# Cross attention of a Perceiver block: the keys computed by seven half-size products and kept in DRAM, in place of scores straight from the context

## The chip, the cores and the metric

The kernel runs on one core of one Trainium2 chip. The metric is the device time of one execution in microseconds (us); times compared are medians of several executions.

## What is computed

The reference is a two-layer model on x (8 batches x 64 rows x 512) with a context of 8 x 1601 rows x 1024. Only this part of it matters here, the cross attention of the second layer (16 heads of 64, one learned null key and value in front of or behind the 1601 others):

```
q      = layernorm(x) @ Wq                      # 512 -> 1024, 16 heads x 64
k, v   = split(context @ Wkv, 2)                # 1024 -> 2 x 1024
k, v   = k, v with the null key / null value    # 1602 keys per batch
p      = softmax(q @ k.T / 8)                   # per batch and head: 64 x 1602
out    = (p @ v) @ Wout
```

Every large product is made of float16 parts: a float32 operand is a high half plus a low half (the rest), and a product is high x high + high x low + low x high, three matmuls.

## The kernel before

The program is a row of stages: depool, Mamba, BitNet, `queries` (stage "cq"), `attend` (stage "ca"), then `project_out`, `head_attention`, `experts`. One engine program stands per stage and engine, in a fixed order, tied by semaphores.

**Values.** V = context @ Wv for all batches is computed ahead, as filler between the work of the early stages (`ValueWork`) and at full width in `queries` (`QuadWork`: two tiles of 128 context rows by the two halves of the width, as seven products of half-size blocks in place of eight, the sums and differences made on GpSimd and VectorE), split into halves and written to DRAM (`vd`). 17 such quads run in `queries`.

**Scores, in `attend`.** The keys are never formed. The loop runs over f = 0 to 63: 8 batches x 8 pairs of heads. `project(f, r)` (L1820 to L1822) multiplies the pair's query by Wk transposed, so that the query is 1024 wide (24 matmuls of 128 columns, moved by L1911 on ScalarE and L1964 on VectorE into `qw`); `chunk(f, n)` (L1841 to L1843) multiplies it with the split context, in four chunks of 448, 448, 353 and 352 keys, eight slices of the width and three matmuls for each: 96 matmuls. The context halves of one batch lie in three rings of `ctx` (`halves` and `ctx`); the tiles of the next batch are loaded (L1750), split on ScalarE (L1905) and on VectorE (L1957) while this one is used. Wk transposed is prepared in `queries` (items "keyw"), and so are the first seven tiles of batch 0 (`load_first`, `first_high`, `first_low`, L701 and L705).

**After the scores**, per pair: `peak_of` and `offset` on VectorE (L1969, L1973: the maximum), `exps` on ScalarE (L1919), `inverse` (L1978, L1981), `weights_high` on ScalarE (L1928), `weights_low` on VectorE (L1986), `turn` on the queue of SyncE (L1769: two DMA transposes of the two halves), and `attend_to` on TensorE (L1870, L1873) with the pair's values, loaded by L1757 and L1759; every fourth pair `leave` (L1995, L1997) moves the sums out of PSUM. `attend_to(f - 2)` stands between the chunks of f, so TensorE has a pair and a half of other work while the weights of a pair are made. `probs` and `parts` have one buffer each, the scores six banks of PSUM.

## Time and profile before

| | us |
|---|---|
| median of 3 runs | 3063.41 (3062.07 to 3064.23) |
| the profiled execution | 3065.92 |
| its span | 3063.9 |
| TensorE busy in the span | 2838.0 (93%) |
| VectorE, ScalarE, GpSimd busy | 1625.4, 1041.0, 248.5 |
| `attend`: first matmul to the last sum moved out | 1331.5 to 2583.9 |
| granted TensorE clock, mean | 0.967 |

The profile is of one execution. PE is TensorE's matmul, PEld its weight load, DVE VectorE, ACT ScalarE, POOL GpSimd, SP SyncE (SPq its queue of DMA issues). A matmul's duration in the trace includes its way through the array, so two that follow each other overlap: what one costs is the distance between two starts. The clock is given in tenths or as a share of full speed (2.4 GHz).

### The profile page before, as it was taken

What the parts mean: (1) busy time and instruction counts of PE and PEld (TensorE: products, weight loads), DVE (VectorE), ACT (ScalarE), POOL (GpSimd) and SP (SyncE); (2) the same over time, 40 slices, a digit from 0 to 9 for tenths busy, and PEclk for the clock granted to TensorE, in tenths of its full rate; (3) what the DMA queues carried; (4) which work ended last, traced back from release to release, by engine and by line L of the source; (5) the groups of instructions that cost most, each with busy time, mean ns of one, the idle gap of its engine ahead of it and who ended that gap; (6) DMA issues with size and microseconds to landing.
All of it is one profiled execution on the core that took longest, in us unless ns stands there. A gap on an engine that the chain in (4) does not pass through costs nothing. (4 is left out here: it accounts for less than half of the span.)

```text
span 3063.9 us, 42939 instructions
## 1 busy us (share of the span) xinstructions
PE 2838.0 (93%) x17913; PEld 1507.4 (49%) x17921; DVE 1625.4 (53%) x1942; ACT 1041.0 (34%) x1621; POOL 248.5 (8%) x338
## 2 busy tenths in 40 slices
PE   6999999998989999989999999999999997786799
PEld 3334444443444444446665666666666664334453
DVE  5358999995565666643434343434343432367410
ACT  2254433431433443332333333333232321173210
POOL 1000000000000555500000000000000000100000
PEclk9999999999999999999999999999999998887899
DMA  5033334334323444345655565555555544100203
GB/s 203 24 108 103 96 108 129 94 97 163 126 83 126 146 128 139 113 129 116 146 117 143 117 149 116 149 115 150 115 150 114 130 86 104 59 7 22 110 21 131
DMA packets 487175, 343.00 MB, mean 112 GB/s; under 512 B 246884, under 2 KB 452005, under 8 KB 482759
## 3 DMA queue, kind: packets, MB, share of 16 engines
q1 hardware_dynamic: 486982, 340.26, 40.8%
q8 instruction: 142, 2.33, 0.3%
q14 instruction: 51, 0.41, 0.0%
HBM read 231.06 MB, written 54.62 MB: 93 GB/s over the span
## 5 line engine op out<-in xcount | busy, mean ns | idle before, releaser
L1841 PE MATMUL ca_p_s<-early_halves,ca_qw 128*128 128x448 f16 (+2 forms) x1408 | 466.7, 331 | 1.4 <-DVE ca_qw L1964 1.4
L1843 PE MATMUL ca_p_s<-early_halves,ca_qw 128*128 128x448 f16 (+2 forms) x1408 | 466.8, 332 | 0.0
L1842 PE MATMUL ca_p_s<-early_halves,ca_qw 128*128 128x448 f16 (+2 forms) x1408 | 466.8, 332 | 0.0
L1964 DVE TENSOR_TENSOR ca_qw<-ca_p_w,ca_qw 128x512 f16<-128x512 f32 x128 | 88.5, 691 | 508.3 <-ACT ca_qw L1911 508.3
L394 PE MATMUL vw_pv<-vw_wv,vw_ctx 128*128 128x512 f16 (+1 forms) x688 | 263.9, 384 | 36.6 <-PEq L74 15.3
L395 PE MATMUL vw_pv<-vw_wv,vw_ctx 128*128 128x512 f16 (+1 forms) x688 | 263.6, 383 | 0.0
L396 PE MATMUL vw_pv<-vw_wv,vw_ctx 128*128 128x512 f16 (+1 forms) x688 | 263.6, 383 | 0.0
L1911 ACT ACTIVATE ca_qw<-ca_p_w 128x512 f16<-128x512 f32 x128 | 76.4, 597 | 504.5 <-PE ca_p_w L1822 504.5
L1842 PE MATMUL ca_p_s<-ca_ctx,ca_qw 128*128 128x448 f16 (+2 forms) x640 | 216.2, 338 | 0.0
L1841 PE MATMUL ca_p_s<-ca_ctx,ca_qw 128*128 128x448 f16 (+2 forms) x640 | 216.1, 338 | 0.0
L1843 PE MATMUL ca_p_s<-ca_ctx,ca_qw 128*128 128x448 f16 (+2 forms) x640 | 216.1, 338 | 0.0
L1919 ACT ACTIVATE ca_probs<-ca_p_s,ca_small 128x896 f32<-128x896 f32 (+1 forms) x128 | 117.6, 924 | 219.5 <-DVE ca_small L1973 219.5
L1843 PEld LDWEIGHTS ca_p_s<-early_halves,ca_qw 128*128 128x128 f16 x1408 | 137.9, 98 | 99.1 <-issue 0.9
L1986 DVE SCALAR_TENSOR_TENSOR ca_parts<-ca_probs,ca_small,ca_parts 128x1602 f16<-128x1602 f32 x64 | 120.8, 1888 | 118.6 <-ACT ca_parts L1928 118.6
L1841 PEld LDWEIGHTS ca_p_s<-early_halves,ca_qw 128*128 128x128 f16 x1408 | 137.8, 98 | 90.5 <-DVE ca_qw L1964 1.7
L1842 PEld LDWEIGHTS ca_p_s<-early_halves,ca_qw 128*128 128x128 f16 x1408 | 137.8, 98 | 88.8 <-issue 0.9
L1248 ACT ACTIVATE work<-early_halves,mb_a_neg 128x252 f32<-128x252 f32 x256 | 104.7, 492 | 219.2 <-DVE ms_h L1281 215.5
L1969 DVE TENSOR_REDUCE ca_small<-ca_p_s 128x1 f32<-128x896 f32 (+1 forms) x128 | 126.5, 988 | 64.3 <-PE ca_p_s L1843 64.3
L394 PE MATMUL ms_pv<-vw_wv,vw_ctx 128*128 128x512 f16 x336 | 129.2, 385 | 16.8 <-DVE vw_ctx L370 8.6
L1281 DVE TENSOR_TENSOR_SCAN ms_h<-work,ms_h 128x2048 f32<-128x2048 f32 x32 | 141.3, 4417 | 0.0
L1806 POOL COPY ca_q_diag<-work 64x128 f16<-64x128 f16 x128 | 43.9, 343 | 1158.7 <-PE ca_p_s L1843 1154.8
L394 PEld LDWEIGHTS vw_pv<-vw_wv,vw_ctx 128*128 128x128 f16 (+1 forms) x688 | 67.7, 98 | 128.5 <-issue 27.5
(554 smaller groups left out, 5356.6 us busy)
## 6 DMA issues: line engine op xcount, KB each, us to landing
ca_stage<-in_ctx_t SPq DMA_DIRECT2D x97, 512.0 KB, 3.6
vd<-vw_vst SPq DMA_DIRECT2D x192, 256.0 KB, 2.3
ca_vals<-vd SPq DMA_DIRECT2D x64, 768.0 KB
vw_ring<-in_ctx_t SPq DMA_DIRECT2D x89, 512.0 KB, 3.8
ex_w_d<-in_w_d SPq DMA_DIRECT2D x8, 2048.0 KB, 7.2
vw_ring<-in_w_kv SPq DMA_DIRECT2D x16, 512.0 KB, 4.7
early_r<-state_rows SPq DMA_DIRECT2D x8, 1024.0 KB, 7.7
early_r<-in_w SPq DMA_DIRECT2D x2, 4096.0 KB, 14.3
```

The source lines that it names most:

```text
L394: self.nc.tensor.matmul(o, xh[:, c, 0:w], self.wv[0][:, c, f], start=(c == 0), stop=False)
L395: self.nc.tensor.matmul(o, xh[:, c, 0:w], self.wv[1][:, c, f], start=False, stop=False)
L396: last = self.nc.tensor.matmul(o, xl[:, c, 0:w], self.wv[0][:, c, f], start=False, stop=(c == CC - 1))
L1248: ins = nc.scalar.activation(da[q][:, m, :, 1:], steps, ACT.Exp, scale=a_neg[:, e, q * NQ + m:q * NQ + m + 1])
L1281: nc.vector.tensor_tensor_scan(flat, da[q].rearrange("p n b s -> p (n b s)"), flat, 0.0, ALU.mult, ALU.add).then_inc(scanned, 1)
L1841: nc.tensor.matmul(o, a[:, 0, c, :], x[:, 0, c, lo:hi], start=(c == 0), stop=False)
L1842: nc.tensor.matmul(o, a[:, 0, c, :], x[:, 1, c, lo:hi], start=False, stop=False)
L1843: last = nc.tensor.matmul(o, a[:, 1, c, :], x[:, 0, c, lo:hi], start=False, stop=(c == CC - 1))
L1919: nc.scalar.activation(probs[:, CUTS[2 * h]:CUTS[2 * h + 2]].rearrange("p (a n) -> p a n", a=2), scores(f, h), ACT.Exp, bias=nbias, scale= ...
L1964: nc.vector.tensor_tensor(qw[f % 2][:, 1, c, :], p_w[:, :].rearrange("p (c n) -> p c n", n=P), qw[f % 2][:, 0, c, :], ALU.subtract).then_i ...
L1969: nc.vector.tensor_reduce(peak[:, h:h + 1], scores(f, h), AX.XY, ALU.max).then_inc(peak_done, 1)
L1986: nc.vector.scalar_tensor_tensor(parts[:, 1, 0:KEYS], probs[:, :], rinv, parts[:, 0, 0:KEYS], ALU.mult, ALU.subtract).then_inc(wl_done, 1)
```

## The change

K itself is computed, in `attend`, by a new class `KeyWork`. A batch's 1602 keys are four quads of two tiles of 201 keys (198 in the last). A quad's K is seven products of half-size blocks instead of eight: each has 4 blocks of 128 features x 4 slices of the width x 3 matmuls of 201 columns, 48 matmuls, so 336 matmuls per quad and 32 quads. GpSimd makes four sums of 804 columns and four low halves per quad, ScalarE seven high halves, VectorE three low halves; the products are added up on VectorE (14 additions of 402 columns) with two copies by ScalarE (`keep`), split (four `out_high`, four `out_low`) and written to DRAM (`kd`). A step t of the new order is half a quad (seven groups of 24 matmuls, `kw.pe`) together with one pair of heads f = t - 9: `load_keys` reads the pair's keys back, `score(f)` is 12 matmuls of 402 (396) columns from the 128-wide query itself, and `attend_to(f - 1)` follows. Products run in steps 0 to 63, pairs in steps 9 to 72. The scores have four banks of PSUM instead of six, the products three. `project`, `chunk`, `null_of`, the splitting of context tiles and the six-bank rotation are gone, and so are "keyw" and the first tiles in `queries`; there a new class `KeyWeights` makes the seven half-size weight blocks in eight steps spread over 16 quads (56 high halves, 56 low halves and 32 subtractions of 256 columns).

The core of the diff:

```diff
+KQ = 4
+KN = 201
+KN_LAST = KEYS // 2 - (KQ - 1) * KN
...
             self.add(dve, i, 0)
+            if step and not later:
+                keys.low_given(dve, s)
+            elif step:
+                keys.low(dve, s, 3)
+                keys.low(dve, s, 4)
+                keys.second(dve, s)
...
+class KeyWeights:
+    ORDER = [0, 3, 5, 2, 4, 1, 6]
+    WIDE = BANK // 2
+    STEPS = CC // 2 * 2
...
+    def low_given(self, dve, s):
+        w11, w12, w21, w22 = self.quarters
+        for n in range(3):
+            self.low(dve, s, n)
+        dve.wait_ge(self.lo, 7 * s + 3)
+        self.nc.vector.tensor_tensor(w11, w12, w11, ALU.subtract).then_inc(self.made, 1)
+        dve.wait_ge(self.made, 4 * s + 1)
+        self.nc.vector.tensor_tensor(w12, w22, w12, ALU.subtract).then_inc(self.made, 1)
...
+class KeyWork:
+    SLOTS = 9
+    STAGED = 3
+    BANKS = 3
+    QUADS = B * KQ
+    HALF = CC // 2
+    WIDE = HALF * KN
+    OF_SUMS = {2: 0, 1: 1, 4: 2, 5: 3}
+    BY_POOL = [1, 2, 4, 5]
+    BY_DVE = [0, 3, 6]
...
+    def load(self, sp, i):
+        if i >= self.QUADS:
+            return
+        if i:
+            sp.wait_ge(self.op_lo, 3 * i)
+            sp.wait_ge(self.s_lo, 4 * i)
+        for t in range(2):
+            sp.dma_start(self.raws[t][:, :, :].rearrange("p h n -> p (h n)"),
+                         self.io.ctx_k[i // KQ, i % KQ, t, :, :]).then_inc(self.ld[t], 16)
...
+        g.tensor_tensor(s[:, 0, :], b[:, 0, :], b[:, 1, :], ALU.add).then_inc(self.s_made, 1)
+        g.wait_ge(self.s_made, 4 * i + 1)
+        g.tensor_tensor(s[:, 1, :], s[:, 0, :], a[:, 0, :], ALU.subtract).then_inc(self.s_made, 1)
+        g.wait_ge(self.s_made, 4 * i + 2)
+        g.tensor_tensor(b[:, 0, :], a[:, 0, :], b[:, 0, :], ALU.subtract).then_inc(self.s_made, 1)
+        g.wait_ge(self.s_made, 4 * i + 3)
+        self.low_of_sum(g, i, 1)
+        g.wait_ge(self.s_lo, 4 * i + 1)
+        self.low_of_sum(g, i, 2)
...
+        g.wait_ge(self.s_lo, 4 * i + 2)
+        self.low_of_sum(g, i, 4)
+        g.wait_ge(self.s_lo, 4 * i + 3)
+        g.tensor_tensor(self.sums[:, 0, :], self.raws[0][:, 1, :], self.sums[:, 1, :], ALU.subtract)\
+            .then_inc(self.s_made, 1)
+        self.low_of_sum(g, i, 5)
...
+    def pe(self, pe, m):
+        i, r, h = m // 14, m % 14 // 2, m % 2
+        if h == 0:
+            if r in self.BY_POOL:
+                pe.wait_ge(self.s_lo, 4 * i + self.BY_POOL.index(r) + 1)
+            else:
+                pe.wait_ge(self.op_lo, 3 * i + self.BY_DVE.index(r) + 1)
+        if m >= self.BANKS:
+            j, q, g = (m - self.BANKS) // 14, (m - self.BANKS) % 14 // 2, (m - self.BANKS) % 2
+            if q:
+                pe.wait_ge(self.added, 14 * j + self.ADD_AT[self.READ[q], g] + 1)
+            else:
+                pe.wait_ge(self.copied, 2 * j + g + 1)
+        w, x, o, n = self.tk[r], self.slot(i, r), self.bank(m), self.wide(i)
+        for e in range(2):
+            f = slice((2 * h + e) * P, (2 * h + e + 1) * P)
+            for c in range(self.HALF):
+                k = slice(c * KN, c * KN + n)
+                self.nc.tensor.matmul(o[:, e, :], w[:, 0, c, f], x[:, 0, k], start=(c == 0), stop=False)
+                self.nc.tensor.matmul(o[:, e, :], w[:, 0, c, f], x[:, 1, k], start=False, stop=False)
+                last = self.nc.tensor.matmul(o[:, e, :], w[:, 1, c, f], x[:, 0, k], start=False, stop=(c == self.HALF - 1))
+        last.then_inc(self.prod, 1)
...
+            def load_keys(f):
+                b, p = divmod(f, PAIRS)
+                if p == 0:
+                    kw.landed(sp, b)
+                if f >= 2:
+                    sp.wait_ge(scored, 2 * (f - 1))
+                o = keys[f % 2]
+                source = kd[b, :, :, p, :, :].rearrange("q t p n -> p (q t) n")
+                sp.dma_start(o[:, 0:2 * KQ - 1, :, :].rearrange("p a l n -> p a (l n)"), source[:, 0:2 * KQ - 1, :])\
+                    .then_inc(ld_k[f % 2], 16)
...
+            for t in range(STEPS):
+                f, (i, later) = t - BEHIND, divmod(t, 2)
+                if t and not later:
+                    kw.load(sp, i + 1)
+                if 0 <= f + 1 < NF:
+                    load_keys(f + 1)
+                if t < PARTS and later:
+                    kw.out(sp, i, 0)
+                if f >= 0:
+                    turn(f, 0)
+                    turn(f, 1)
+                if t < PARTS and later:
+                    kw.out(sp, i, 1)
+                    kw.out(sp, i, 2)
+                if 2 <= f + 1 < NF:
+                    load_values(f + 1)
+                if t < PARTS and later:
+                    kw.out(sp, i, 3)
...
+            def score(f):
                 pe.wait_ge(q_ready, 2 * f + 2)
-                if 2 * f + r:
-                    pe.wait_ge(qw_low, 2 * f + r)
-                p, q = f % PAIRS, q_diag[f % 2]
-                for i in range(CC // 2):
-                    c = (r * CC // 2 + i) * P
-                    o = p_w[:, i * P:(i + 1) * P]
-                    nc.tensor.matmul(o, wkt[0][:, p, c:c + P], q[:, 0, :], start=True, stop=False)
-                    nc.tensor.matmul(o, wkt[0][:, p, c:c + P], q[:, 1, :], start=False, stop=False)
-                    last = nc.tensor.matmul(o, wkt[1][:, p, c:c + P], q[:, 0, :], start=False, stop=True)
-                last.then_inc(qw_ready, 1)
-            def chunk(f, n):
-                b, h = f // PAIRS, n // 2
-                if n % 2 == 0:
-                    if 2 * f + h >= 3:
-                        pe.wait_ge(exp_done, 2 * f + h - 2)
-                    if n == 0:
-                        pe.wait_ge(qw_low, 2 * f + 2)
-                    if f % PAIRS == 0 and (b or h):
-                        pe.wait_ge(ctx_low, HERE + (b - 1) * JT + (JT if h else EARLY))
-                if n == 2:
-                    null_of(f)
-                x = ctx[(2 * b + h) % 3]
-                lo, hi = CUTS[n] - h * HALF_KEYS, min(CUTS[n + 1], CTX) - h * HALF_KEYS
-                o = bank(f, n)[:, 0:hi - lo]
-                a = qw[f % 2]
-                for c in range(CC):
-                    nc.tensor.matmul(o, a[:, 0, c, :], x[:, 0, c, lo:hi], start=(c == 0), stop=False)
-                    nc.tensor.matmul(o, a[:, 0, c, :], x[:, 1, c, lo:hi], start=False, stop=False)
-                    last = nc.tensor.matmul(o, a[:, 1, c, :], x[:, 0, c, lo:hi], start=False, stop=(c == CC - 1))
-                if n % 2:
-                    last.then_inc(half_done, 1)
-            def null_of(f):
+                pe.wait_ge(ld_k[f % 2], 32 * (f // 2 + 1))
                 if f == 0:
-                    pe.wait_ge(null_low, 1)
-                at = CTX - CUTS[3]
-                o, q = bank(f, 3)[:, at:at + 1], q_diag[f % 2]
-                nc.tensor.matmul(o, q[:, 0, :], nk_parts[:, 0:1], start=True, stop=False)
-                nc.tensor.matmul(o, q[:, 0, :], nk_parts[:, 1:2], start=False, stop=False)
-                nc.tensor.matmul(o, q[:, 1, :], nk_parts[:, 0:1], start=False, stop=True)
+                    pe.wait_ge(key_set, 2)
+                else:
+                    pe.wait_ge(exp_done, 2 * f)
+                q, x = q_diag[f % 2], keys[f % 2]
+                for n in range(KQ):
+                    w = KN if n < KQ - 1 else KN_LAST
+                    o = p_s[:, n * BANK:n * BANK + 2 * w].rearrange("p (a n) -> p a n", n=w)
+                    nc.tensor.matmul(o, q[:, 0, :], x[:, 2 * n:2 * n + 2, 0, 0:w], start=True, stop=False)
+                    nc.tensor.matmul(o, q[:, 0, :], x[:, 2 * n:2 * n + 2, 1, 0:w], start=False, stop=False)
+                    last = nc.tensor.matmul(o, q[:, 1, :], x[:, 2 * n:2 * n + 2, 0, 0:w], start=False, stop=True)
+                    if n >= KQ - 2:
+                        last.then_inc(scored, 1)
...
+            for t in range(STEPS + 1):
+                f = t - BEHIND
+                if 0 <= f < NF:
+                    score(f)
+                if t < PARTS:
+                    for n in range(3):
+                        kw.pe(pe, 7 * t + n)
+                if f >= 1:
+                    attend_to(f - 1)
+                if t < PARTS:
+                    for n in range(3, 7):
+                        kw.pe(pe, 7 * t + n)
...
+            for t in range(STEPS):
+                f, (i, later) = t - BEHIND, divmod(t, 2)
+                if t < PARTS and not later:
+                    kw.keep(act, i, 0)
+                    kw.keep(act, i, 1)
+                if f >= 0:
+                    exps(f)
+                    weights_high(f)
+                if t < PARTS and not later:
+                    kw.high(act, i + 1, 0)
+                    kw.high(act, i + 1, 1)
+                    kw.high(act, i + 1, 2)
+                elif t < PARTS:
+                    kw.out_high(act, i, 0)
+                    kw.high(act, i + 1, 3)
+                    kw.high(act, i + 1, 4)
+                    kw.out_high(act, i, 1)
+                    kw.high(act, i + 1, 5)
+                    kw.out_high(act, i, 2)
+                    kw.high(act, i + 1, 6)
+                    kw.out_high(act, i, 3)
...
+                if 0 <= f < NF:
+                    peak_of(f)
+                if quad and later:
+                    kw.add(dve, i, 2, 1)
+                if 0 <= f < NF:
+                    inverse(f)
+                if quad and later:
+                    kw.add(dve, i, 3, 0)
+                    kw.add(dve, i, 4, 0)
+                if 0 <= f < NF:
+                    weights_low(f)
+                if quad and not later:
+                    kw.add(dve, i, 0, 0)
+                    kw.add(dve, i, 0, 1)
+                    kw.low(dve, i + 1, 0)
+                    kw.add(dve, i, 1, 0)
+                    kw.add(dve, i, 1, 1)
+                    kw.add(dve, i, 2, 0)
+                elif quad:
+                    kw.add(dve, i, 3, 1)
+                    kw.add(dve, i, 4, 1)
+                    kw.out_low(dve, i, 0)
+                    kw.low(dve, i + 1, 3)
+                    kw.out_low(dve, i, 1)
+                    kw.add(dve, i, 5, 0)
+                    kw.add(dve, i, 5, 1)
+                    kw.out_low(dve, i, 2)
+                    kw.low(dve, i + 1, 6)
+                    kw.add(dve, i, 6, 0)
+                    kw.add(dve, i, 6, 1)
+                    kw.out_low(dve, i, 3)
+                if f >= 1 and (f - 1) % GP == GP - 1:
+                    leave((f - 1) // GP)
...
```

How the order moves, at two places on which the waits turn. VectorE, before, one pair of heads (L1969 the maxima of the two halves, L1964 the low half of the widened query, L1957 a context tile, L1986 the low half of the weights):

```order
L1969 TENSOR_REDUCE ca_small<-ca_p_s 128x1
L1964 TENSOR_TENSOR ca_qw<-ca_p_w,ca_qw 128x512
L1957 TENSOR_TENSOR ca_ctx<-ca_stage,ca_ctx 128x8x128
L1969 TENSOR_REDUCE ca_small<-ca_p_s 128x1
L1973 TENSOR_SCALAR ca_small<-ca_small 128x1
L1964 TENSOR_TENSOR ca_qw<-ca_p_w,ca_qw 128x512
L1978 TENSOR_SCALAR ca_small<-ca_small 128x1
L1981 RECIPROCAL ca_small<-ca_small 128x1
L1986 SCALAR_TENSOR_TENSOR ca_parts<-ca_probs,ca_small,ca_parts 128x1602
```

VectorE, changed, an odd step with a pair (L2170 the maxima, L1898 the additions of products, L2187 the low half of the weights, L1918 the low half of a finished block of K, L1849 the low half of an operand):

```order
L2170 TENSOR_REDUCE ca_small<-ca_p_s 128x1 x2
L2172 TENSOR_SCALAR ca_small<-ca_small 128x1
L1898 TENSOR_TENSOR ca_held<-ca_p_k,ca_held 128x2x198
L2177 TENSOR_SCALAR ca_small<-ca_small 128x1
L2180 RECIPROCAL ca_small<-ca_small 128x1
L1898 TENSOR_TENSOR ca_held<-ca_p_k,ca_held 128x2x198 x2
L2187 SCALAR_TENSOR_TENSOR ca_parts<-ca_probs,ca_small,ca_parts 128x1602
L1898 TENSOR_TENSOR ca_held<-ca_p_k,ca_held 128x2x198 x2
L1918 TENSOR_TENSOR ca_k_out<-ca_held,ca_k_out 128x4x198
L1849 TENSOR_TENSOR ca_slot<-early_region,ca_slot 128x804
L1918 TENSOR_TENSOR ca_k_out<-ca_held,ca_k_out 128x4x198
L1898 TENSOR_TENSOR ca_held<-ca_p_k,ca_held 128x2x198 x2
```

The additions, which free the products' banks, now stand in one queue with the chain of the weights, the last pair shown behind three operations of the splitting. The queue of SyncE, before, one pair:

```order
L1769 DMA_TRANSPOSE ca_turned<-ca_parts 128x13x128 x2
L1757 DMA ca_vals<-vd 128x12x256
L1759 DMA ca_vals<-vd 65x256
L1750 DMA ca_stage<-in_ctx_t 128x1024
L1769 DMA_TRANSPOSE ca_turned<-ca_parts 128x13x128 x2
```

and changed, an odd step and the start of the even one behind it (L1980, L1982 keys read back, L1925 blocks of K out, L2002 the transposes, L1781 a quad's context):

```order
L1980 DMA ca_keys<-kd 128x7x402
L1982 DMA ca_keys<-kd 128x2x197
L1925 DMA kd<-ca_k_out 128x4x402
L2002 DMA_TRANSPOSE ca_turned<-ca_parts 128x13x128 x2
L1925 DMA kd<-ca_k_out 128x4x402 x2
L1991 DMA ca_vals<-vd 128x12x256
L1993 DMA ca_vals<-vd 65x256
L1925 DMA kd<-ca_k_out 128x4x402
L1781 DMA early_region<-in_ctx_k 128x1608 x2
L1980 DMA ca_keys<-kd 128x7x402
```

The context of the next quad and the next pair's keys are now behind the last block of K of the quad.

## Rows read from the trace of the kernel before

**Rows 1.** The page's 40 slices of the span, in tenths.

```profile
PE   6999999998989999989999999999999997786799
...
PEclk9999999999999999999999999999999998887899
```

**Rows 2.** Busy time in stretches (us, PE, PEld, DVE, ACT, POOL busy, PEclk, DMA share, GB/s).

```profile
1010.00:1327.00 317.00, 313.56 (x1452) 142.01 (x1452) 206.52 (x248) 123.00 (x214) 175.42 (x136) 1.00 0.43 125
1331.40:2584.00 1252.60, 1226.82 (x11200) 765.77 (x11200) 489.06 (x643) 396.83 (x548) 43.37 (x126) 0.99 0.55 127
1660.00:2500.00 840.00, 833.99 (x7621) 520.90 (x7619) 334.03 (x439) 269.99 (x373) 30.40 (x88) 1.00 0.55 128
```

**Rows 3.** Timeline of TensorE: start, us, line, one matmul each; L1870 two.

```profile
1702.21 0.22 PE L1820 MATMUL ca_p_w<-ca_q_diag,early_r 128*128 128x128 f16 x1
...
1702.88 0.31 PE L1841 MATMUL ca_p_s<-ca_ctx,ca_qw 128*128 128x352 f16 x1
...
1706.48 0.35 PE L1841 MATMUL ca_p_s<-early_halves,ca_qw 128*128 128x448 f16 x1
...
1711.02 0.22 PE L1820 MATMUL ca_p_w<-ca_q_diag,early_r 128*128 128x128 f16 x1
...
1716.32 0.25 PE L1870 MATMUL ca_p_o<-ca_turned,ca_vals 128*64 128x128 f16 x2
...
1717.58 0.18 PE L1852 MATMUL ca_p_s<-ca_nk_parts,ca_q_diag 128*128 128x1 f16 x1
```

**Rows 4.** Waits within `attend`: us in total, times, longest us.

```profile
PE ca_p_s L1852 <- ACT ca_probs L1919: 11.5, 7, 2.8
```

**Rows 5.** Timeline of TensorE at the stage's start.

```profile
1331.45 0.29 PE L1820 MATMUL ca_p_w<-ca_q_diag,early_r 128*128 128x128 f16 x1 [6.66 <-POOL ca_q_diag L1806]
```

**Rows 6.** Timeline at the stage's end, VectorE.

```profile
2569.28 0.89 DVE L1969 TENSOR_REDUCE ca_small<-ca_p_s 128x1 f32<-128x706 f32 x1 [7.55 <-PE ca_p_s L1843]
...
2574.68 1.89 DVE L1986 SCALAR_TENSOR_TENSOR ca_parts<-ca_probs,ca_small,ca_parts 128x1602 f16<-128x1602 f32 x1 [1.85 <-ACT ca_parts L1928]
...
2583.43 0.42 DVE L1997 SCALAR_TENSOR_TENSOR work<-ca_p_o,work 128x256 f32<-128x256 f32 x1
```

**Rows 7.** The same, TensorE.

```profile
2580.64 0.32 PE L1870 MATMUL ca_p_o<-ca_turned,ca_vals 128*64 128x128 f16 x2 [10.14 <-DMA ca_turned<-ca_parts]
```

**Rows 8.** Groups of VectorE by shape, 1000 to 2600 us: busy us, mean ns.

```profile
L1986 DVE SCALAR_TENSOR_TENSOR ca_parts<-ca_probs,ca_small,ca_parts 128x1602 f16<-128x1602 f32 x64 | 120.8, 1888 | 118.6 <-ACT ca_parts L1928 118.6
...
L691 DVE TENSOR_TENSOR vw_vst<-cq_held,vw_vst 128x512 f16<-128x512 f32 x68 | 76.2, 1121 | 35.5 <-ACT vw_vst L686 35.5
...
L1969 DVE TENSOR_REDUCE ca_small<-ca_p_s 128x1 f32<-128x896 f32 x64 | 69.3, 1083 | 1.8 <-PE ca_p_s L1843 1.8
...
L677 DVE TENSOR_TENSOR cq_held<-cq_p_q,cq_held 128x512 f32<-128x512 f32 x79 | 54.3, 687 | 28.3 <-PE cq_p_q L751 27.4 <-issue 0.3
```

**Rows 9.** Groups of ScalarE, the same stretch.

```profile
L1928 ACT ACTIVATE ca_parts<-ca_probs,ca_small 128x1602 f16<-128x1602 f32 x64 | 104.4, 1631 | 73.2 <-DVE ca_small L1981 73.2
...
L1919 ACT ACTIVATE ca_probs<-ca_p_s,ca_small 128x896 f32<-128x896 f32 x64 | 64.5, 1007 | 219.5 <-DVE ca_small L1973 219.5
```

**Rows 10.** Groups of GpSimd, the same stretch.

```profile
L638 POOL TENSOR_TENSOR vw_ctx<-cq_sums,vw_ctx 128x512 f16<-128x512 f32 x41 | 47.8, 1174 | 71.7 <-ACT vw_ctx L647 71.7
```

**Rows 11.** Timeline of VectorE in `queries`.

```profile
1180.93 1.72 DVE L691 TENSOR_TENSOR vw_vst<-cq_held,vw_vst 128x512 f16<-128x512 f32 x1 [0.70 <-ACT vw_vst L686]
```

**Rows 12.** Timeline of GpSimd, the same moment.

```profile
1180.83 1.27 POOL L625 TENSOR_TENSOR cq_sums<-cq_sums,vw_ring 128x512 f32<-128x512 f32 x1
```

**Rows 13.** DMA queues at the stage's end, 2574.6 to 2580.6 (two transposes alone).

```profile
q1 hardware_dynamic: 3392, 0.85, 76.3%
```

**Rows 14.** DMA, 1330 to 1345, 40 slices, GB/s.

```profile
GB/s 0 0 0 3 109 76 164 306 459 382 393 371 470 350 382 459 328 330 350 348 315 289 291 288 291 289 291 288 292 291 298 372 328 393 382 437 415 393 437 393
```

**Rows 15.** DMA queues, 1660 to 2500.

```profile
q1 hardware_dynamic: 229896, 106.08, 55.0%
```

**Rows 16.** Weight loads, groups by shape, 1010 to 2600.

```profile
L1822 PEld LDWEIGHTS ca_p_w<-ca_q_diag,early_r 128*128 128x128 f16 x512 | 50.5, 99 | 0.0
```

503 lines of the change are left out of this document (283 added, 220 removed).

## The prediction

> **What bounds the kernel now.** I read the page's slices first, then the stretches, then the stage that the change rewrites, instruction by instruction. TensorE is at nine tenths or more in nearly all slices, at full clock, until the last stages [rows 1]. In `attend` it is busy 1226.8 of 1252.6 us, so 25.8 us are idle; VectorE (489 us), ScalarE (397) and GpSimd (43) have room, and the DMA engines stand at 0.55 [rows 2]. So this stage ends with TensorE's own work, and what a matmul costs is the distance between starts: 12 matmuls of 128 columns take 0.67 us (56 ns each), 24 of 352 columns 3.60 us (150 ns), 24 of 448 columns 4.54 us (189 ns), and a pair's `attend_to` 1.35 us with the gaps around it [rows 3].
>
> **The change, part by part.**
>
> *TensorE's work.* Removed per pair: 24 x 56 ns = 1.34 us of `project`, 48 x 189 + 48 x 150 ns = 16.28 us of `chunk`, 0.09 us for the null column: 17.71 us. Added per step: 168 matmuls of 201 (a quarter of them 198) columns. The line through the three sizes is 56 ns + 0.42 ns per column above 128, so 86.6 and 85.4 ns: 14.50 us, 2.07 us for each group of 24. The scores are 12 of 402 (396) columns, 170 ns each: 2.04 us. Together 16.54 us, 1.17 us less, over 64 pairs **-75 us**. Weight loads show 99 ns each [rows 16], yet 128-column matmuls with one each follow at 56 ns, so loads are hidden there and should be at 86 ns.
>
> *Idle time of before.* All 25.8 us go: 11.5 us are waits for the exponentials [rows 4], some 10 us the wait for the last transposes [rows 7], the rest lies at the start: **-25.8 us**. What is late in its place follows.
>
> *Start.* The first matmul came at 1331.45 [rows 5]. Now it needs the first context tile of 0.82 MB, loaded only when the stage begins: at 390 GB/s [rows 14] 2.1 us and about as much again for issue and landing, then a high and a low half of 804 columns (0.9 and 1.0 us). That is 5.5 us later, and GpSimd's first sums (below) cost about 1: **+6.5**.
>
> *Steps with a pair* (55 steps, t = 9 to 63, 27.5 quads). TensorE needs 16.54 + 1.35 = 17.9 us a step. Costs beside it, scaled by columns: an addition of 402 columns from PSUM 687 x 402/512 = 0.54 us; a low half of 804 columns between 0.95 and 1.08, I take 1.0; the two maxima 1083/896 x 1602 and a start, 2.0; low weights 1.89 [rows 8]; high weights 1.63, exponentials 1007/896 x 1602 and a second start, 2.1 [rows 9]; a GpSimd operation 1174 x 804/512 = 1.84 us [rows 10], eight per quad, 15 of 36 us. VectorE has per quad 14 additions, 7 low halves, 2 x 4.6 us for the pairs: 24 of 36 us. Sum of busy time is no limit, but order is. In the odd step, from its start: maxima from 1.6 (three of four banks), bias at 3.9, exponentials 6.0, inverse 6.5, high weights 8.1, low weights 10.1, two additions 11.3, three low halves 14.3, the addition of product 5 14.9. TensorE wants that bank for its seventh group at 15.8. Margin 0.9 us. But each of the three reads two SBUF operands while GpSimd works on sums: one such operation took 1.72 us, begun 0.1 us behind a GpSimd operation of 1.27 us [rows 11, 12], while 687 ns is the undisturbed cost, and the group's mean is 1121 [rows 8]. Three delays of up to 1.84 us make -0.9 to +4.6 us; one full delay, near the mean of those 68, gives 1.0 us of stall. In the even step the exponentials stand behind ScalarE's second copy (6.8), the first addition ends at 13.5 and is wanted at 13.7, with its backlog I take 0.3. So 1.3 us per quad: **+36** (0 to 95).
> The Trainium skill ("GPSIMD Engine Reference", Specifications) says that the interfaces are shared with VectorE, with contention for VectorE instructions that have two SBUF inputs. It speaks against this change, which multiplies both kinds; by that rule alone, with a full wait each time, the sum would be at its upper bound of 95; the trace agrees on the kind (1121 against 687 ns) and shows that the full wait is not the rule.
>
> *DMA.* A pair's two transposes alone took 76.3% of 6 us, 4.6 us of all engines [rows 13]. Values are 0.82 MB at 289 GB/s (512-byte rows, the plateau in [rows 14]): 2.8 us. Keys read back, 0.82 MB, and K written, 0.82 MB, in pieces of 804 bytes, I price the same: 2.8 each. Context 0.82 MB at 390: 2.1. Sum 15.2 us a step. The same sum for before is 9.5 of 19.1 us, 50%, where 55% are shown [rows 15]; so about 16.9 of 17.9 us now, 94%. I count nothing, but the cover is thin: context and keys of an even step are issued 5 us into it, behind the last block of K, and land at about 15 to 16, wanted at 17.9.
>
> *Drain.* With the products over at step 63, nine pairs remain (9 x 2.04 us of scores, ten times 1.35 of `attend_to`, 31.9 us of work) on single buffers of `probs` and `parts`. One pair's ring: maxima 2.3, exponentials 2.1, inverse 0.5, weights 1.6 + 1.9, 8.5 us. DMA per pair 4.6 + 2.8 + 2.8 = 10.2 us, which is longer. Before, from the last score to the end were 14.6 us [rows 6], now with the score and the longer maximum 17.4. So 8 x 10.2 + 17.4 = 99 us, less the work: **+67** (54 to 85).
>
> *`queries`.* TensorE idles 3.4 of 317 us there, VectorE is at 65% [rows 2]. 15 pairs of splittings go, 56 + 32 operations of 256 columns (0.34 to 0.41 us) come on VectorE: 36 - 18 us, 71%. Six banks give slack of two products and more; the context of the next weights is loaded only at a quad's end, which holds up ScalarE. **+3** (0 to 15).
>
> Sum: -75 - 25.8 + 6.5 + 36 + 67 + 3 = +12 us. The profiled execution, 3065.92, becomes 3078; it lies 2.5 us above the median, so the median becomes **3075 us**.
>
> **The rivals.**
> 1. *VectorE stays ahead of TensorE (faster).* Place: the addition of product 5 in the odd step. If the three low halves before it cost at most 1.3 us each, the 0.9 us margin holds, the 36 us vanish, and with a ring of 8.6 us in the drain another 13: 3027. It decides at 0.9 us of stall per quad: below it the kernel is faster. For it: most single L691 run at 0.69. Against: GpSimd is busy just there, with the low half of product 4, the fourth sum and the low half of product 5.
> 2. *The DMA engines become the bound.* If pieces of 804 and 394 bytes go at less than the plateau, a step takes 20 us in place of 17.9 + 0.65: 55 x 1.45 = +80: 3155. For it: 94%, one queue in order. Against: whether shares near 1 lengthen anything is not seen in the steady stretch of before.
> 3. *Deeper stalls of both engines' order*: 3.5 us per quad, +60: 3135.
> 4. *Weight loads bound short matmuls.* If a matmul of 201 columns followed at the load's 99 ns instead of 86: 13 x 168 x 64 = +140 us, 3215. Against: 56 ns at 128 columns [rows 3]. The Trainium skill ("TensorE: Matmul & The Clock Gate", Back-to-back issue gap) gives about 81 ns per matmul at 128 columns in streams of loads and matmuls, and 131 ns at 512; this trace has 56 at 128.
>
> **How the numbers follow.** A measurement of this kernel tells about 0.2%, 6 us, from no change. The forecast's case (3055 to 3100) has 0.40, of which 0.12 lies within 6 us of before and 0.02 below. Rival 1, from 3020 to 3055, 0.34; rival 2 0.12; rival 3 0.10; rival 4 0.02; the rest, 0.02, that the saving in matmuls is not there. Faster 0.36, same 0.12, slower 0.52. The range is 3020 to 3145: it takes in rival 1 with all bounds at their low ends, the forecast and rival 3, and leaves out most of rival 2 and all of 4. Since both signs hold much, the forecast's own range is 3055 to 3100.
>
> **What would show it.** Groups of matmuls of 201 columns starting 2.07 us apart; steps without a pair at 14.5 us; gaps of about 1 us on TensorE before the seventh group of odd steps, released by the addition on VectorE; steps with a pair 18.5 us in the mean; a DMA share above 0.85 there; after the last product about 100 us with TensorE a third busy. I am wrong if that drain is near 60 or above 130 us, if gaps are released by DMAs (keys, context), if TensorE shows no gaps, or if `queries` grows by over 15 us.

## The result and the profile after

The changed kernel takes **3158.44 us** (median of 4, 3156.91 to 3159.66) where the kernel before takes 3063.82 on the same chip: ratio **1.0306**, 95% interval 1.0288 to 1.0324. Slower, as forecast as the likelier sign, but by 95 us and not by 12, and outside the range. The span of the profiled execution is 3156.2 us, 92.3 more than before.

The page's slices (granted clock and DMA engines):

```profile
PE   6999999988989988879999999999999974696799
PEclk9999999999999999989999999999999986797899
DMA  5133343343324333333599999999999989201203
```

Beside [rows 1], TensorE has 8, 8, 8, 7 in slices 15 to 18, which are `queries`, where it had 9, 9, 9, 8, and the DMA engines stand at nine tenths through the steps with a pair. The stretches (columns: window, length, busy time and count of PE, PEld, DVE, ACT, POOL, then granted clock, DMA share, GB/s): `queries`, the gap before the first product of K, the first step, the rest up to the first pair, most of the steps with a pair, the drain, and all stages behind:

```profile
1010.00:1368.00 358.00, 327.31 (x1433) 142.13 (x1431) 246.67 (x323) 131.54 (x259) 178.06 (x134) 0.95 0.34 104
1368.00:1382.40 14.40, 0.00 (x0) 0.00 (x0) 4.20 (x6) 2.13 (x3) 0.00 (x0) 0.63 0.64 187
1382.40:1409.00 26.60, 18.38 (x171) 17.20 (x172) 7.53 (x11) 6.73 (x11) 22.20 (x16) 0.82 0.33 102
1409.00:1540.00 131.00, 121.68 (x1361) 119.04 (x1359) 71.08 (x86) 40.64 (x54) 66.51 (x36) 0.99 0.39 119
1540.00:2571.00 1031.00, 996.83 (x12704) 924.92 (x12702) 703.45 (x934) 469.05 (x630) 472.42 (x326) 1.00 0.94 218
2571.00:2683.50 112.50, 49.67 (x620) 29.20 (x618) 42.49 (x61) 32.15 (x46) 4.32 (x14) 0.63 0.91 201
2683.50:3156.00 472.50, 378.03 (x1440) 189.23 (x1440) 191.18 (x370) 138.71 (x247) 18.78 (x36) 0.88 0.17 62
```

Read against [rows 2], the time from 1010 us on goes as follows (all in us):

| stretch | forecast | measured | miss |
|---|---|---|---|
| up to the first product of K (before: up to 1331.45) | +8.5 (5.5 start, 3 `queries`) | +51.0 (1382.41) | +42.5 |
| nine steps without a pair | 131.5 | 155.2 | +23.7 |
| steps with a pair | 1020.5 (55 x 17.9 + 36) | 1031.7 | +11.2 |
| drain: last product to the last sum moved out | 99 | 114.0 | +15.0 |
| stages behind | 480.1 | 472.8 | -7.3 |

The misses add to 85 us; the span missed by 80, since the parts as forecast add up to 5 us less than the forecast (rounding and small gaps). Half lies up to the first product. By the medians the miss is 83 us, 95 measured against 12 forecast.

**`queries`.** The waits there, ScalarE's and TensorE's (engine, line, whom for: us in all, times, longest):

```profile
ACT early_r L817 <- DMA early_region<-in_w_kv: 39.8, 7, 6.3
DVE vw_ctx L631 <- ACT vw_ctx L625: 45.4, 20, 7.7
PE cq_p_q L713 <- DVE cq_held L655: 20.6, 9, 5.1
PEld cq_p_q L713 <- DVE cq_parts L631: 11.4, 3, 5.3
PE vw_pv L713 <- DVE cq_held L655: 9.8, 5, 4.5
```

Before, TensorE had one wait of 2.2 us in this stretch. Now it is a chain: `high_given` (L817), in ScalarE's fixed order, waits seven times for the next step's key weights, 5.7 us each in the mean; behind it stand the high halves of the next quad, on them VectorE's low halves (L631), behind those the additions (L655) that free TensorE's banks. Six of the seven reach TensorE as waits of 3.5 to 5.1 us. And it is paid twice. Four stretches of 20 us (same columns), then one of the waits and what follows it:

```profile
1130.00:1150.00 20.00, 19.71 (x91) 8.61 (x89) 13.12 (x18) 5.81 (x11) 9.46 (x7) 1.00 0.40 119
1150.00:1170.00 20.00, 15.63 (x60) 6.56 (x61) 14.10 (x19) 7.35 (x15) 10.41 (x8) 0.83 0.25 83
1170.00:1190.00 20.00, 20.00 (x95) 9.01 (x93) 15.80 (x21) 8.40 (x17) 10.91 (x8) 1.00 0.36 114
1190.00:1210.00 20.00, 15.13 (x58) 6.03 (x57) 11.43 (x16) 6.04 (x12) 6.69 (x6) 0.83 0.38 119
```
```profile
1149.84:1154.36 4.52, 0.00 (x1) 0.03 (x1) 1.43 (x3) 2.59 (x6) 0.87 (x1) 0.87 0.62 235
1154.36:1160.00 5.64, 5.63 (x14) 2.01 (x15) 4.84 (x8) 1.17 (x3) 1.58 (x2) 0.50 0.00 1
1160.00:1165.00 5.00, 5.00 (x25) 2.26 (x24) 4.22 (x6) 2.28 (x4) 3.48 (x3) 1.00 0.26 73
```

In the two stretches where TensorE waits 4.4 and 4.9 us of 20, the granted clock is 0.83, and it issues 60 and 58 matmuls instead of 91 to 95. The order is seen in the last fence: the clock falls while TensorE stands in the wait, the next 5.6 us of full work go at 1.2 GHz (14 matmuls of 512 columns), and then the clock is back at 2.4 (25 in 5 us). Each of the six waits is followed by such a stretch, 37 us at the lower clock in all.

**A step with a pair.** VectorE in the odd step whose first product starts at 2142.47 (start, duration, then in brackets what was waited for), and GpSimd beside it:

```profile
2142.15 1.89 DVE L2170 TENSOR_REDUCE ca_small<-ca_p_s 128x1 f32<-128x1206 f32 x2 [0.89 <-PE ca_p_s L2081]
...
2148.53 1.89 DVE L2187 SCALAR_TENSOR_TENSOR ca_parts<-ca_probs,ca_small,ca_parts 128x1602 f16<-128x1602 f32 x1 [0.52 <-issue]
2150.34 1.05 DVE L1898 TENSOR_TENSOR ca_held<-ca_p_k,ca_held 128x402 f32<-128x402 f32 x2
2151.31 2.17 DVE L1918 TENSOR_TENSOR ca_k_out<-ca_held,ca_k_out 128x804 f16<-128x804 f32 x1
2153.40 2.67 DVE L1849 TENSOR_TENSOR ca_slot<-early_region,ca_slot 128x804 f16<-128x804 f32 x1
2156.00 0.98 DVE L1918 TENSOR_TENSOR ca_k_out<-ca_held,ca_k_out 128x804 f16<-128x804 f32 x1
2156.90 1.05 DVE L1898 TENSOR_TENSOR ca_held<-ca_p_k,ca_held 128x402 f32<-128x402 f32 x2
```
```profile
2150.91 1.72 POOL L1832 TENSOR_TENSOR ca_slot<-early_region,ca_slot 128x804 f16<-128x804 f32 x1 [3.17 <-ACT ca_slot L1841]
2152.70 2.52 POOL L1824 TENSOR_TENSOR ca_sums<-early_region,ca_sums 128x804 f32<-128x804 f32 x1
2156.27 2.28 POOL L1832 TENSOR_TENSOR ca_slot<-ca_sums,ca_slot 128x804 f16<-128x804 f32 x1 [1.05 <-ACT ca_slot L1841]
```

Of the three low halves two are drawn out to 2.17 and 2.67 us while GpSimd works, the third takes 0.98; the addition of product 5 begins at 2156.90, and TensorE's seventh group starts 1.1 us late. The place and nearly the size are the forecast's, and so is the cause, as experiment 3 will show: over 27 odd steps 1.26 us each (forecast 1.0), in even steps 0.3 (forecast 0.3), and the step 18.73 us in the mean from the second score to the 55th (forecast 18.5). Groups of 24 matmuls start 2.05 to 2.10 us apart (forecast 2.07).

**The drain.** From the last product to the last matmul are 112.9 us (the measure used below); the scores start 11.2 us apart in the mean (9.5 to 9.8 and 12.9 to 13.6 in turn). The queue of SyncE, and TensorE's waits from 2560 to 2690 us:

```profile
2605.14 5.34 SPq L2002 DMA_TRANSPOSE ca_turned<-ca_parts  x2
2610.54 1.01 SPq L1991 DMA_DIRECT2D ca_vals<-vd  x1
2611.61 0.72 SPq L1993 DMA_DIRECT2D ca_vals<-vd  x1
2612.37 0.36 SPq L1980 DMA_DIRECT2D ca_keys<-kd  x1
2612.78 1.40 SPq L1982 DMA_DIRECT2D ca_keys<-kd  x1
```
```profile
PE ca_p_s L2079 <- DMA ca_keys<-kd: 30.2, 5, 13.8
PE ca_p_o L2099 <- DMA ca_turned<-ca_parts: 16.8, 5, 7.9
```

The keys of the next pair are issued behind the transposes and the values, and the first wait, 13.8 us, is for the last K to be written and read back.

### The profile page after: what moved, and what is told of

Same layout as the page of the kernel before. It is cut to its first block and busy times, and to the rows that moved or that the text cites. A ratio compares the mean times of both kernels' runs of the same rounds, so it can differ in the third digit from the quotient of the medians.

```text
span 3156.2 us, 52755 instructions
## 1 busy us (share of the span) xinstructions
PE 2806.2 (89%) x21569; PEld 1830.7 (58%) x21569; DVE 1997.1 (63%) x2464; ACT 1198.2 (38%) x1853; POOL 775.1 (25%) x597
## 5 line engine op out<-in xcount | busy, mean ns | idle before, releaser
L1873 PE MATMUL ca_p_k<-early_region,early_r 128*128 128x201 f16 (+1 forms) x1376 | 346.6, 252 | 24.6 <-DVE early_region L1849 14.5
L1874 PE MATMUL ca_p_k<-early_region,early_r 128*128 128x201 f16 (+1 forms) x1376 | 343.9, 250 | 0.0
L1875 PE MATMUL ca_p_k<-early_region,early_r 128*128 128x201 f16 (+1 forms) x1376 | 343.8, 250 | 0.0
L1898 DVE TENSOR_TENSOR ca_held<-ca_p_k,ca_held 128x402 f32<-128x402 f32 (+1 forms) x448 | 241.3, 567 | 121.1 <-PE ca_p_k L1875 121.1
L1873 PE MATMUL ca_p_k<-early_region 128*128 128x201 f16 (+1 forms) x1024 | 257.7, 252 | 22.9 <-DVE ca_held L1898 22.9
L1874 PE MATMUL ca_p_k<-early_region 128*128 128x201 f16 (+1 forms) x1024 | 255.5, 250 | 0.0
L1875 PE MATMUL ca_p_k<-early_region 128*128 128x201 f16 (+1 forms) x1024 | 255.5, 250 | 0.0
L1918 DVE TENSOR_TENSOR ca_k_out<-ca_held,ca_k_out 128x804 f16<-128x804 f32 (+1 forms) x128 | 165.6, 1294 | 61.9 <-ACT ca_k_out L1914 61.9
L1303 ACT ACTIVATE work<-early_region,mb_a_neg 128x252 f32<-128x252 f32 x256 | 104.7, 492 | 219.1 <-DVE ms_h L1336 215.4
L1808 POOL TENSOR_TENSOR ca_sums<-early_region 128x804 f32<-128x804 f32 x32 | 61.6, 1925 | 480.1 <-DMA early_region<-in_ctx_k 480.1
L2187 DVE SCALAR_TENSOR_TENSOR ca_parts<-ca_probs,ca_small,ca_parts 128x1602 f16<-128x1602 f32 x64 | 120.8, 1888 | 81.8 <-ACT ca_parts L2136 67.8
L1873 PE MATMUL ca_p_k<-ca_slot,early_r 128*128 128x201 f16 (+1 forms) x672 | 168.4, 251 | 0.2 <-DVE ca_held L1898 0.2
L1874 PE MATMUL ca_p_k<-ca_slot,early_r 128*128 128x201 f16 (+1 forms) x672 | 167.2, 249 | 0.0
L1875 PE MATMUL ca_p_k<-ca_slot,early_r 128*128 128x201 f16 (+1 forms) x672 | 167.1, 249 | 0.0
L1914 ACT ACTIVATE ca_k_out<-ca_held 128x804 f16<-128x804 f32 (+1 forms) x128 | 111.7, 873 | 143.4 <-DVE ca_held L1898 143.3
L2170 DVE TENSOR_REDUCE ca_small<-ca_p_s 128x1 f32<-128x1206 f32 (+1 forms) x128 | 120.7, 984 | 61.8 <-PE ca_p_s L2081 61.8
L2127 ACT ACTIVATE ca_probs<-ca_p_s,ca_small 128x1206 f32<-128x1206 f32 (+1 forms) x128 | 117.6, 925 | 105.6 <-DVE ca_small L2172 105.0
L1873 PEld LDWEIGHTS ca_p_k<-early_region,early_r 128*128 128x128 f16 x1376 | 133.8, 97 | 30.3 <-DVE early_region L1849 15.0
```

The lines of the kernel that those rows point to most:

```text
L1873: self.nc.tensor.matmul(o[:, e, :], w[:, 0, c, f], x[:, 0, k], start=(c == 0), stop=False)
L1874: self.nc.tensor.matmul(o[:, e, :], w[:, 0, c, f], x[:, 1, k], start=False, stop=False)
L1875: last = self.nc.tensor.matmul(o[:, e, :], w[:, 1, c, f], x[:, 0, k], start=False, stop=(c == self.HALF - 1))
L1898: self.nc.vector.tensor_tensor(self.part(out, h, w), self.bank(m), self.part(other, h, w), ALU.add)\
L1914: self.nc.scalar.activation(self.out_place(i, k, 0), self.result(i, k), ACT.Copy).then_inc(self.out_hi, 1)
L1918: self.nc.vector.tensor_tensor(self.out_place(i, k, 1), self.result(i, k), self.out_place(i, k, 0), ALU.subtract)\
```

## The experiments

Most are single edits of the changed kernel; each quoted text names a theory and a rival. Each run has its own runs of the kernel before beside it, so I compare ratios; 0.001 is 3.1 us, and each ratio is known to about 0.002. "Less" and "more" below are against the changed kernel unless another is named. "Steps" are the mean distance from the second score to the 55th of the profiled execution, "period" the mean distance of two scores in the drain. The changed kernel stands at 1.0306.

**1. The key weights' load, earlier** (L567).

```diff
                         .then_inc(self.v_out[k], 16)
-            if i % 2:
-                self.keys.load(sp, i // 2 + 1)
+                if i % 2 and k == 1:
+                    self.keys.load(sp, i // 2 + 1)
```

> The changed kernel, with the load of the next step's key weights issued after the second of an odd quad's four outputs instead of after the fourth; nothing else. Theory (ScalarE's in-order queue is held by that transfer: it waits for it 39.8 us in `queries`, 7 times, up to 6.3 us, and TensorE then waits, 46 us in all): the transfer is issued some 5 us earlier, ScalarE's wait shrinks to under 8 us in all, TensorE's idle time in `queries` from 30 us to under 10, its clock there stays at full, and the time falls by 30 to 42 us, to about 3120. Rival (VectorE is simply overloaded there by the 56 low halves and 32 differences, 58 us of new work): ScalarE's wait shrinks but TensorE waits for VectorE as before, and the time falls by under 10 us.

3111.92 us, ratio 1.0148 (1.0133 to 1.0163): 48 us less. The stretches up to the end of `queries` and the gap:

```profile
1010.00:1333.00 323.00, 317.75 (x1457) 140.40 (x1454) 247.80 (x324) 132.47 (x262) 181.04 (x136) 1.00 0.40 122
1333.00:1347.60 14.60, 0.02 (x1) 0.00 (x0) 4.51 (x7) 2.33 (x4) 0.00 (x0) 0.63 0.63 186
```

TensorE is idle 5 us instead of 31, at full clock, and the first product of K comes 34.8 us earlier. Theory upheld: not VectorE's work, which is all still there. What remains to before is 8 us in `queries` (323 against 315) and 8 in the gap. Of the 35 us, 25 are idle time and 10 are TensorE's own work done at full clock. The whole time fell by more than the expected 30 to 42 us: in the traces another 12 us lie between the first product and the last, where this edit changes nothing; e4 and e7, which change only the drain, have 8 and 7 us less there too. So the trace gives this cause 35 us; what shortened the other stretch is open.

**2. The addition of product 5 ahead of the low halves.**

```diff
                     kw.add(dve, i, 4, 1)
+                    kw.add(dve, i, 5, 0)
                     kw.out_low(dve, i, 0)
                     kw.low(dve, i + 1, 3)
                     kw.out_low(dve, i, 1)
-                    kw.add(dve, i, 5, 0)
```

> The changed kernel, with VectorE's addition of product 5, first half, moved ahead of the three low halves in the odd step; nothing else. Theory (the addition's place behind the three low halves is what TensorE's last group of the odd step waits for, 1.26 us per odd step in 27 steps): that wait falls below 0.3 us, steps with a pair go from 18.73 to about 18.2 us, the time falls by 25 to 32 us, to about 3130. Rival (VectorE is behind as a whole, so the wait only moves to the next group, which waits for the addition of the second half): the steps stay within 0.2 us of 18.7 and the time falls by under 8 us.

3195.61 us, ratio 1.0425 (1.0405 to 1.0445): 37 us **more**. The odd step's wait went as expected, but the even step grew from 18.3 to 21.1 us. VectorE in the odd step ahead of such an even one:

```profile
2175.14 0.58 DVE L1898 TENSOR_TENSOR ca_held<-ca_p_k,ca_held 128x402 f32<-128x402 f32 x1 [1.09 <-PE ca_p_k L1875]
2175.64 2.47 DVE L1918 TENSOR_TENSOR ca_k_out<-ca_held,ca_k_out 128x804 f16<-128x804 f32 x1
2178.03 0.98 DVE L1849 TENSOR_TENSOR ca_slot<-early_region,ca_slot 128x804 f16<-128x804 f32 x1
2178.93 2.50 DVE L1918 TENSOR_TENSOR ca_k_out<-ca_held,ca_k_out 128x804 f16<-128x804 f32 x1
```

It stands idle 1.09 us for the product, and then meets GpSimd as before; the backlog reaches the next step's maxima and the writing of K. Both theory and rival fell: the wait did move, as the rival said, but at a loss.

**3. GpSimd's work on K nearly gone.** Its eight operations per quad work on 64 of 804 columns from the sixth quad on; K is left uncomputed in the others. One of the eight:

```diff
-        g.tensor_tensor(s[:, 0, :], b[:, 0, :], b[:, 1, :], ALU.add).then_inc(self.s_made, 1)
+        g.tensor_tensor(s[:, 0, n], b[:, 0, n], b[:, 1, n], ALU.add).then_inc(self.s_made, 1)
```

> The changed kernel, with GpSimd's eight operations per quad of K on 64 of 804 columns from the sixth quad on (K is then wrong in the other columns; everything else is computed as before). Theory (the stalls exist because VectorE's operations with two SBUF operands are held up by GpSimd's): the low halves of K fall from 1.29 us and 1.6 us to about 1.0 us, the wait before the seventh group of odd steps vanishes, steps with a pair come to about 18.0 us, and the time falls by 35 to 45 us, to about 3118. Rival (the order alone makes the stalls): the low halves get shorter but at least 0.8 us of the 1.26 us stays, and the time falls by under 15 us.

3121.51 us, ratio 1.0179 (1.0162 to 1.0196): 39 us less, as the theory had it (35 to 45). VectorE's low halves in the steps with a pair, in the changed kernel (first fence) and here (its lines stand five lower); columns: busy, mean ns, idle before:

```profile
L1918 DVE TENSOR_TENSOR ca_k_out<-ca_held,ca_k_out 128x804 f16<-128x804 f32 (+1 forms) x105 | 134.4, 1280 | 50.0 <-ACT ca_k_out L1914 50.0
L1849 DVE TENSOR_TENSOR ca_slot<-early_region,ca_slot 128x804 f16<-128x804 f32 x26 | 42.4, 1633 | 0.6 <-ACT ca_slot L1841 0.5
```
```profile
L1923 DVE TENSOR_TENSOR ca_k_out<-ca_held,ca_k_out 128x804 f16<-128x804 f32 (+1 forms) x104 | 102.7, 988 | 49.1 <-ACT ca_k_out L1919 49.1
L1854 DVE TENSOR_TENSOR ca_slot<-early_region,ca_slot 128x804 f16<-128x804 f32 x26 | 26.8, 1031 | 0.3 <-ACT ca_slot L1846 0.3
```

From 1.28 and 1.63 us to 0.99 and 1.03, no wait left before the seventh group, steps of 18.06 us. GpSimd's work, not the order alone, makes the stall. The same view shows the additions, which have one operand in PSUM, at 567 and 569 ns with and without GpSimd: that agrees with the Trainium skill ("GPSIMD Engine Reference", Specifications), which names VectorE instructions with two SBUF inputs, beside those in a 2-port performance mode, as the ones that contend with GpSimd.

**4. In the drain, keys ahead of the transposes.**

```diff
-                if 0 <= f + 1 < NF:
+                if 0 <= f + 1 < NF and t < PARTS + 2:
                     load_keys(f + 1)
+                if t > PARTS and f + 2 < NF:
+                    load_keys(f + 2)
```

> The changed kernel, with the keys of pair f + 2 loaded, in the steps after the last product, ahead of the transposes of pair f instead of behind them and the values; nothing else. Theory (in the drain a score waits for keys that stand behind the transposes and the values in the one queue: 30.2 us of waits, 5 times): the period of a pair falls from 11.4 us to the 8.5 to 9.5 us of the ring of maxima, exponentials and weights, the time falls by 12 to 20 us. Rival (the DMA engines, 91% busy there, set the period: 10.2 us per pair): the wait moves from the keys to the transposes, the period is 10.2 to 11.4 us, the time falls by 0 to 9 us.

3145.69 us, ratio 1.0251 (1.0228 to 1.0274): 17 us less by the ratios, of which the drain shows 10. It fell from 112.9 to 102.7 us, the period from 11.2 to 9.9:

```profile
PE ca_p_o L2101 <- DMA ca_turned<-ca_parts: 37.3, 8, 7.1
PE ca_p_s L2081 <- DMA ca_keys<-kd: 17.4, 2, 12.7
```
```profile
2579.00:2659.00 80.00, 42.51 (x512) 26.73 (x512) 34.50 (x51) 27.82 (x40) 3.50 (x12) 0.71 1.09 245
```

The waits moved to the transposes and the DMA share is full (1.09; the view adds up the transfers' own times, so it can pass 1): in mechanism the rival, the DMA engines. In size neither: the period is under the rival's 10.2 us and above the theory's 9.5.

**7. The same, with the last seven pairs' values hardly loaded** (`load_values`; those pairs use old values).

```diff
+                if f >= NF - PAIRS + 1:
+                    for n in range(2):
+                        sp.dma_start(v[0:LAST, n * FULL, :, :].rearrange("p l f -> p (l f)"),
...
+                    return
```

> The kernel of e4 (keys ahead of the transposes once the products are over), and for the last seven pairs the loads of values cut to two blocks of 65 rows (those pairs then use old values; everything else is as before). Theory (the DMA engines set the period of about 9.9 us in e4's drain: 10.2 us per pair by my prices): 2.8 us per pair go, the period falls to the ring's 8.5 to 8.8 us, the drain from 103 to about 94 us, the time by 7 to 11 us below e4's. Rival (the ring of score, maximum, exponentials and weights, with matmuls at the low clock, sets 9.9 us by itself): the period and the time stay within 3 us of e4's.

3142.11 us, ratio 1.0260 (1.0241 to 1.0280): in the whole time not to be told from e4. In the trace the drain is 96.4 us and the period 9.0:

```profile
2575.00:2655.00 80.00, 43.46 (x512) 26.47 (x512) 36.19 (x52) 28.47 (x40) 3.48 (x12) 0.69 0.87 190
```

With the DMA engines at 0.87 the period falls by 0.9 us, not by their 2.8. So the DMA engines did set e4's period, and another limit stands 0.9 us behind them; its 9.0 us are near the 8.5 to 8.8 expected of the ring of score, maximum, exponentials and weights, which was not tried by itself. Two limits close together.

**5. E2's order, with the context's load ahead of K's last block.**

```diff
-                if t and not later:
-                    kw.load(sp, i + 1)
...
                 if t < PARTS and later:
+                    kw.load(sp, i + 2)
                     kw.out(sp, i, 3)
```

> The kernel of e2 (addition of product 5, first half, ahead of the low halves), and the context tiles of the quad after the next issued ahead of the last block of K in the odd step, instead of after it in the even one. In e2 the odd step's wait went, but waits of 0.5 and 0.7 us came in each even step, where VectorE's low half of the next quad stands ahead of four additions and waits, through ScalarE, for the context (ScalarE 3.0 us there). Theory (the queue of transfers is held behind VectorE's last low half, and the late context then holds VectorE): with the context issued earlier those waits vanish, steps with a pair come to 18.0 to 18.3 us, the time is 25 to 45 us below that of the changed kernel, about 3120. Rival (VectorE has too much work beside GpSimd whatever the order): steps stay above 18.6 us and the time within 10 us of the changed kernel's.

3222.42 us, ratio 1.0515 (1.0493 to 1.0538): 28 us worse than e2. Neither theory nor rival held; the steps grew to 20.07 us. The queue shows why it is worse than e2, at a batch's first pair:

```profile
2158.73 1.43 SPq L1781 DMA_DIRECT2D early_region<-in_ctx_k  x2
2160.20 0.47 SPq L1925 DMA_DIRECT2D kd<-ca_k_out  x1
2170.19 0.38 SPq L1980 DMA_DIRECT2D ca_keys<-kd  x1
```

The last block of K, now behind the context, is 10 us on its way (6.8 in the changed kernel), and the keys of the new batch must wait for it: the step ahead of a first pair took 24.1 us in the mean (20.5 in e2), the one behind it 20.1 (18.1). The other even steps stayed at 20.8 us (21.3 in e2), so e2's own backlog was hardly touched.

**6. The first quad's sums and low halves on VectorE.**

```diff
-            for r in kw.BY_DVE:
-                kw.low(dve, 0, r)
+            kw.low(dve, 0, 0)
+            kw.sums_first(dve, 0)
+            kw.low(dve, 0, 3)
+            kw.sums_second(dve, 0)
+            kw.low(dve, 0, 6)
```

> The changed kernel, with the eight sums and low halves that GpSimd makes for the first quad of K made by VectorE, which is idle then. Theory (the first step took 26.4 us instead of 14.5 because GpSimd's chain of 1.9 us operations feeds the second product on): the chain shrinks to 1.0 us an operation, the first step takes 15 to 19 us, and the time falls by 7 to 12 us. Rival (the low clock after the stage's start and the arrival of the context make that step long): the step stays above 22 us and the time falls by under 4 us.

3147.23 us, ratio 1.0274 (1.0257 to 1.0292), 10 us less. The first step took 20.4 us, from 26.4: 6 us were GpSimd's chain. Groups of 3.9, 4.3 and 3.8 us remain, in a stretch that begins at the low clock. The step lies between theory and rival, the gain within the theory's 7 to 12 us.

**8. E1, e4, e5 and e6 together.**

> The edits of e1, e4, e5 and e6 together. If each gain is in its own stretch they add: 46 (e1, measured), 13 (e4, measured), 25 to 45 (e5, expected) and 7 to 12 (e6, expected) below the changed kernel's 3158, 3042 to 3067 us: as fast as the kernel before, 3063, or faster by up to 20. Rival (a nearer limit, the DMA engines at 0.94 in the steps with a pair, takes over once the stalls are gone): steps stay at 18.5 us and the time is 3075 or more.

3167.83 us, ratio 1.0335 (1.0311 to 1.0359). E5's order takes back all the others give (steps of 20.05 us).

**9. Another order for VectorE.** In the odd step the addition of product 5 goes behind one low half; in the even step work goes into VectorE's waits; and (not shown) the context's load goes ahead of K's last block, except at a batch's end:

```diff
+                if i and i % KQ and quad and not later:
+                    kw.out_low(dve, i - 1, 3)
                 if 0 <= f < NF:
                     inverse(f)
...
+                elif quad:
+                    kw.add(dve, i, 0, 0)
                 if 0 <= f < NF:
                     weights_low(f)
...
                     kw.out_low(dve, i, 0)
+                    kw.add(dve, i, 5, 0)
                     kw.low(dve, i + 1, 3)
```

> The changed kernel with another order of VectorE's work in the steps, of the same operations: in the odd step the addition of product 5, first half, stands behind one low half instead of three (in e2 it stood ahead of all and VectorE waited for the product 1.1 us); in the even step the last low half of K stands behind the maxima, where VectorE waited 2.0 to 2.6 us for the exponentials, and the first addition ahead of the low weights, where it waited 1.8 us for ScalarE (but the low half of K's last block stays where it is at the end of a batch, whose keys wait for it); the context goes ahead of the last block of K, but at a batch's end. Theory (the stall is set by how much of VectorE's in-order queue lies between a step's start and the addition, and e2 and e5 failed because the same queue was already late in the even step and K's last block became late for the keys): the odd step's 1.26 us falls to under 0.3, the even steps gain none, steps with a pair come to 18.1 to 18.3 us, the time falls by 20 to 33 us. Rival (VectorE's whole round of 36 us per quad is full, with GpSimd's delays): steps stay at 18.6 us or above.

3136.00 us, ratio 1.0231 (1.0208 to 1.0254): 23 us less. No wait for VectorE is left in the steps, with GpSimd as busy as before. But steps are 18.39 us, not 18.1 to 18.3; a wait stands before the odd scores, which the view ties to nothing it shows (the line takes in the drain; the steps with a pair have 22 of the 26, 16.3 us, up to 2.0 each):

```profile
PE ca_p_s L2081 <- issue: 32.6, 26, 5.0
```

**10 and 11. E1, e4 and e6; the same with e9.**

> The edits of e1, e4 and e6 together, with the order of VectorE in the steps as in the changed kernel. Theory (each gain is in its own stretch and they add): 46 + 13 + 11 us below the changed kernel's 3158, 3084 to 3094 us. Rival (they share a cause, the clock): less than 60 us below it, above 3098.

> The edits of e1, e4, e6 and e9 together. Theory: e10's time less e9's gain, 3055 to 3072 us, within 0.4% of the kernel before. Rival (e9 gives nothing): 3084 or above.

E10: 3105.61 us, ratio 1.0134 (1.0112 to 1.0157); e11: 3084.24, ratio 1.0069 (1.0045 to 1.0094). They are 22 and 25 us above what the single gains add up to, past the rival's bound and on it. That sum is itself loose: it takes in four or five ratios, and the changed kernel's two or three times over, so I estimate its error at 16 and 22 us from their intervals. Stretch by stretch e10's trace has every gain: 34 us up to the first product, 8 in the first step, 11 in the drain. Two reasons for the rest are seen in the traces. The profiled execution of the changed kernel has 18.73 us a step, where e1, e4, e6 and e7, which do not touch the steps, have 18.62 to 18.69: some 2 to 6 us may have been counted as each edit's gain. And the stages behind, the same code, took 474.0 us there and 479.9 in e10.

**12. Keys ahead of K's last block, in e9** (`early_keys`: the next even step's, but not a batch's first pair).

```diff
                 if t < PARTS and later:
...
+                    if early_keys(f + 2):
+                        load_keys(f + 2)
                     kw.out(sp, i, 3)
```

> The kernel of e9, with the keys of an even step's successor issued ahead of the last block of K instead of behind it (not for the first pair of a batch, whose keys need that block). In e9 TensorE no longer waits for VectorE in the steps, but before the scores of odd steps, 0.75 us each (18.75 against 18.01 us). Theory (those keys stand in the queue behind the last block of K, which waits for VectorE's last low half, and a transfer's issue then takes 4.2 us): the wait vanishes, steps with a pair come to 18.0 to 18.1 us, TensorE's own work, and the time falls by 15 to 22 us below e9's. Rival (the DMA engines are at their limit, some 0.95 of the time, so the order of issue moves nothing): steps stay at 18.3 us or above and the time within 6 us of e9's.

3128.83 us, ratio 1.0195 (1.0174 to 1.0217); the mean step is 18.43 us, as long as e9's. By the mean, and by a gain over e9 of 7 us (11 by the ratios) where 15 to 22 were expected, the rival would stand. The distances between scores, 53 of them in a row, say otherwise (worked out from the starts of L2087; the first 18):

```
18.40 18.08 18.09 18.08 17.77 17.77 20.36 19.75 18.09 18.08 19.01 18.08 17.77 17.77 21.11 19.75 18.08 18.08
```

Most ordinary steps are at TensorE's own 18.08 (17.77 for the narrow quad) with the DMA engines 0.98 busy; what is left stands mostly beside each batch's first pair, whose keys wait for the last block of K. (The profiled execution is the slowest of five, which reach from 3119 to 3137 us.)

**13. All of it** (e1, e4, e6, e12; in the last batch the pairs whose K is written first go first, their keys waiting for all but the last block).

```diff
+        def pair_of(f):
+            b, p = divmod(f, PAIRS)
+            return b, (p + GP) % PAIRS if b == B - 1 else p
```

> The edits of e1, e4, e6 and e12 together, and in the last batch the four pairs whose K is written first are taken first, their keys loaded without waiting for the last block. Theory: e11's 3084 less 15 to 20 us for e12 and 3 to 5 us for the shorter wait at the drain's start (12.5 us in all runs so far): 3059 to 3066 us, the time of the kernel before within 0.2%. Rival (the DMA engines at their limit in the steps): 3078 or above.

3068.48 us (12 runs), ratio **1.0006** (0.9994 to 1.0018): no difference to the kernel before that these runs can tell. Steps 18.27 us, drain 99.6.

**14. Every batch from the pairs that are ready first.**

```diff
-            return b, (p + GP) % PAIRS if b == B - 1 else p
+            return b, (p + GP) % PAIRS
```

> The kernel of e13, with every batch (not the last alone) taken from the four pairs whose K is written first, their keys loaded without waiting for the batch's last block of K. In e12 and e13 the steps between scores are 18.08 or 17.77 us except beside a batch's first pair, where they are 19.3 to 21.1 us, seven times. Theory (the order of issue and the landing of that block, not the DMA engines, which are 98% busy, is what is left): those steps fall to under 18.6 us, the mean from 18.27 to about 18.05 us, the time by 8 to 13 us, to 3055 to 3061, 0.2 to 0.4% below the kernel before. Rival (the DMA engines at their limit): other steps grow in their place, the mean stays at 18.2 us or above and the time within 3 us of e13's.

3080.17 us, ratio 1.0061 (1.0045 to 1.0076). That is 12 us more than e13 where 8 to 13 less were expected. The first pairs' steps are at 18.08, but the two after them at 19 to 20 (mean 18.40, so other steps did grow, as the rival had it), and TensorE waits for VectorE again:

```profile
PE ca_p_k L1873 <- DVE ca_held L1898: 12.1, 21, 1.3
```

The wait for K's landing now stands earlier in the one queue, ahead of the transposes, which VectorE's low weights wait for. That reading was not tried by itself, and the DMA engines, at 0.97 of the time, are not ruled out here. Of the 13.9 us between the two profiled spans only 4.3 lie between first and last product; 3.8 lie ahead and 5.9 in the stages behind, in the same code.

## Why the prediction was wrong, point by point

1. *"`queries` +3 (0 to 15)"*: **the step that failed**. The stage grew by 43 us (358 against 315), beyond the 15 that the prediction gave as a sign of being wrong. It saw that the load "holds up ScalarE" and gave it a few us because six banks give slack. But the slack is in TensorE's banks, and the held engine feeds VectorE, which frees them: of ScalarE's 5.7 us, seven times, 3.5 to 5.1 us reached TensorE six times. The clock then added to it. E1 shows the cause, with 35 of the 43 us. VectorE's new work, priced at 36 us, measured 58 (low halves of 256 columns 0.77 and 0.84 us in the mean; single ones do take the 0.41 of the forecast), and cost 8 us at most.
2. *"Start +6.5"*: the gap was 8 us longer than before and not 5.5, and the first step took 11 us more than the 15.5 forecast, half by GpSimd's chain (e6: 6 us). The stretch began at the low clock, which I had not priced. Odd steps without a pair have the same stall as those with one (6.4 us in four steps); the forecast had them free.
3. *"Steps with a pair +36"*: right in place, engine and size (1.26 + 0.3 against 1.0 + 0.3 per quad). E3 and e9 show its two roots: GpSimd's delays, and an order that puts three low halves ahead of the addition (e9 also moved the context's load, so its gain is not the order's alone). The prediction's own bounds do not agree: three full delays, 4.6 + 0.3 us, would be 135 us over 27.5 quads, while its upper bound of 95 is 3.5 us per quad. E2 shows that the order could not be mended by that one move.
4. *"Drain +67"*: 15 us short. The DMA price of 10.2 us per pair was good (9.9 with the queue in order, e4); of its eight distances between scores the first measured 17.2 us (the wait of 13.8 us for the last K, for which it had no term) and the other seven 11.2 (the keys' place in the queue, 1.3 us per pair by e4); that is 14 of the 15 us.
5. *TensorE's work -75*: groups at 2.05 to 2.10 us, e3's steps at 18.06 against the 17.9 forecast. Right within 0.2 us a step, which over 55 steps is still 9 of the 11 us by which the steps with a pair missed.
6. The rivals: the time measured is close to rival 2's 3155, but by luck and not by its mechanism: steps were 18.73 us, not 20, and e12's ordinary steps run at 18.08 us with the DMA engines at 0.98. Rivals 1 and 4 are out as the kernel stands, and so is rival 3 (1.56 us per quad, not 3.5). E9 takes away TensorE's waits for VectorE, rival 1's mechanism, but not with its time.

Of the 95 us against the kernel before, the causes found, taken together, account for all but 2 (e13), though the edits' single gains add up to more. The steps' stall and most of the drain the forecast had counted; the wait in `queries`, the slow start and the stalls ahead of the first pair it had nearly left out, and they are 66 of the 85 us of misses in the table.

## What to carry to other kernels

A wait placed in an in-order queue costs what stands behind it there, through every engine that is fed from it: follow the chain to the one that frees the busy engine's buffers before calling slack. Moving an operation ahead pays only where its input is already there; otherwise the engine waits, and the backlog comes out in the next step. When gains are added up, compare each stretch of the traces, since single executions of the same code differ by several us in stretches with idle time.

## What was not expected of the hardware

Waits of 3.5 to 5.1 us of TensorE in `queries`, six of them in 260 us, were each followed by a stretch at 1.2 GHz, so that 25 us more of idle time cost 35 up to the first product. The DMA engines ran at a share of 0.98 in the steps of e3 and e12, where ordinary steps still took 18.06 to 18.08 us, TensorE's own time, but a transfer of K begun behind two of context was 10 us on its way instead of 6.8 (at six batch ends, 9.4 to 11.5 us until the keys behind it went out, against 6.8 to 7.7). The stages behind the attention, unchanged in all runs, took 473.3 to 481.4 us.
